# Unread dense 128x128 products between the small tile products of a delta-rule solve

## What is computed

```python
def step(S, inp):
    qt, kt, vt, at, gkt = inp
    Sp = S * jnp.exp(gkt)[..., None]
    u = jnp.einsum('bhk,bhkv->bhv', at, Sp) + vt
    S = Sp + jnp.einsum('bhk,bhv->bhkv', kt, u)
    o = jnp.einsum('bhk,bhkv->bhv', qt, S)
    return (S, o)
```

## Time and profile before

| | us |
|---|---|
| median of 3 runs (lowest 2097.86, highest 2100.38) | 2097.92 |
| the profiled execution's own time | 2104.22 |
| its span, first to last instruction | 2102.4 |
| PE busy in the span | 1794.7 |
| DVE busy | 1135.7 |
| ACT busy | 661.8 |
| POOL busy | 299.7 |
| mean granted clock of PE, as a share of 2.4 GHz | 0.853 |

### The profile page before, as it was taken

The page is one execution under the profiler, slowest core; times in us unless marked ns, Lnnn a source line. Parts: engine busy times, 40 slices in busy tenths (PEclk is TensorE's granted clock), DMA queues, the critical chain, the costliest instruction groups (busy, mean ns, idle before and its releaser), DMA issues. The chain is left out here.

```text
span 2102.4 us, 50203 instructions
## 1 busy us (share of the span) xinstructions
PE 1794.7 (85%) x21793; PEld 1575.6 (75%) x21793; DVE 1135.7 (54%) x2562; ACT 661.8 (31%) x1296; POOL 299.7 (14%) x302
## 2 busy tenths in 40 slices
PE   5677776899999999999999997788777877677589
PEld 4466665689888999999999995577666766666468
DVE  3745554765555455555555565555255246434885
ACT  3344444423223232322223222433223233222232
POOL 0323222700000000000000003312121121110440
PEclk9789887999999999999999997866576577555589
DMA  3100000100000000001010000000000000001001
GB/s 136 48 2 1 0 0 14 70 1 21 21 21 21 21 21 12 30 3 39 1 41 1 1 1 33 1 2 3 3 2 2 3 3 2 3 3 45 1 1 48
DMA packets 9937, 35.91 MB, mean 17 GB/s; under 512 B 3056, under 2 KB 5896, under 8 KB 7176
## 3 DMA queue, kind: packets, MB, share of 16 engines
q1 hardware_dynamic: 9736, 32.96, 4.5%
HBM read 30.47 MB, written 2.49 MB: 16 GB/s over the span
## 5 line engine op out<-in xcount | busy, mean ns | idle before, releaser
L1042 ACT ACTIVATE hidden<-bank,moe_b 128x512 f32<-128x512 f32 (+1 forms) x320 | 213.3, 668 | 537.1 <-PE bank L934 522.7
L951 PE MATMUL bank<-moe_w2h,hidden_hi 128*128 128x256 f32 x1216 | 345.7, 284 | 0.0
L951 PE MATMUL bank<-moe_w2l,hidden_hi 128*128 128x256 f32 x1216 | 344.1, 283 | 0.0
L951 PE MATMUL bank<-moe_w2h,hidden_lo 128*128 128x256 f32 x1216 | 344.0, 283 | 0.0
L934 PE MATMUL bank<-x_hi,moe_w1h 128*128 128x512 f32 (+1 forms) x640 | 243.7, 381 | 2.8 <-ACT hidden L1042 2.7
L934 PE MATMUL bank<-x_lo,moe_w1h 128*128 128x512 f32 (+1 forms) x640 | 242.5, 379 | 0.0
L934 PE MATMUL bank<-x_hi,moe_w1l 128*128 128x512 f32 (+1 forms) x640 | 242.0, 378 | 0.0
L951 PEld LDWEIGHTS bank<-moe_w2h,hidden_hi 128*128 128x128 f32 x1216 | 233.1, 192 | 5.9 <-DVE residual L1076 4.3
L951 PEld LDWEIGHTS bank<-moe_w2l,hidden_hi 128*128 128x128 f32 x1216 | 233.2, 192 | 1.2
L951 PEld LDWEIGHTS bank<-moe_w2h,hidden_lo 128*128 128x128 f32 x1216 | 233.2, 192 | 0.0
L1076 DVE SCALAR_TENSOR_TENSOR residual<-bank,gates,residual 128x256 f32<-128x256 f32 x152 | 73.4, 483 | 290.4 <-PE bank L951 290.4
(11 more groups left out here) (286 smaller groups left out, 3634.3 us busy)
## 6 DMA issues: line engine op xcount, KB each, us to landing
moe_w<-in_moe_w SPq DMA_DIRECT2D x16, 1024.0 KB, 4.8
patches<-in_patches SPq DMA_DIRECT2D x8, 864.0 KB, 4.6
out<-residual SPq DMA_DIRECT2D x19, 128.0 KB, 1.7
ffn_w<-in_ffn_w SPq DMA_DIRECT2D x2, 1024.0 KB, 6.5
att_w<-in_att_w SPq DMA_DIRECT2D x1, 1536.0 KB, 6.1
delta_w<-in_delta_w SPq DMA_DIRECT2D x1, 1280.0 KB
tok_w<-in_tok_w SPq DMA_DIRECT2D x1, 768.0 KB, 4.1
delta_wvf<-in_delta_wvf SPq DMA_DIRECT2D x1, 272.0 KB
```

What stands on the lines that cost most here:

```text
L951: mm = nc.tensor.matmul(bank[4 + n % 3][:, 0:D], left, right, start=(i == 0), stop=(i == len(passes) - 1))
L1042: nc.scalar.activation(H[:, i % 4, 0:n], bank[i % 4][:, 0:n], ACT.Relu, bias=b1[:, x, f:f + 1]).then_inc(acted, 1)
```

## The change

Function `dense(n)` is new. Where the call has a chunk c, and after every fourth lane (n % 4 == 3), it issues one bf16 product of the 128x128 identity against 208 columns (16 columns of the identity, 13 times over), written into columns 304 to 511 of bank 4, which nothing reads. It is called behind each lane of `first_half`, `remainder` and `second_half` but the last of the 32. Two waits on `d_exp` are new, before `first_half` and before `remainder`.

```diff
+            def dense(n):
+                if c is not None and n % 4 == 3:
+                    nc.tensor.matmul(bank[4][:, CT:512], identb[:, :], spread(identb[:, 0:16], 1, 13),
+                                     start=True, stop=True)
+
             def first_half(j):
                 if z is None:
                     return
+                if c is not None:
+                    pe.wait_ge(d_exp, 3)
                 pe.wait_ge(t_back, 3)
                 for lane in lanes(j):
                     for e in range(2):
...
+                    if lane != lanes(j)[-1]:
+                        dense(lane)
                 mm.then_inc(u1_done, 1)
 
             def remainder(j):
                 if z is None:
                     return
                 pe.wait_ge(u1_back, j + 1)
+                if c is not None:
+                    pe.wait_ge(d_exp, 5)
                 for lane in lanes(j):
...
+                    if lane != lanes(j)[-1]:
+                        dense(lane)
                 mm.then_inc(r_done, 1)
 
             def second_half(j):
...
+                    if lane != lanes(j)[-1]:
+                        dense(lane)
                 mm.then_inc(u2_done, 1)
```

## The result

The changed kernel takes **2201.94 us** (median of 4 runs, 2198.26 to 2203.12) against 2098.77 for the kernel before (2097.86 to 2100.38, one run more than in the table above): 1.049 times as long, 95% interval 1.047 to 1.051, or 103 us more. The forecast was 2183, with 2122 to 2214 as its range. The profiled execution took 2203.12 us, 98.9 more than the one of before.

A forecast was written before the change was run, and what follows sets the result against it. PE alone was taken to bound the kernel from first_half to each call's end. Products of 118 us, less 15 of pauses and 18 of clock, gave 85 over 2104.22: 2189, less 6.3 for the median, 2183 us, range 2122 to 2214.

The forecast's parts named there:

- What bounds: From first_half to the call's end (30 us) PE alone is the path; time added there lengthens the kernel.
- The price of a product: Between tiles at 1.2 GHz: entry 0.15, streaming 0.173, exit 0.13, less a pair's 0.054, 0.40 us; at 2.4 GHz 0.30.
- The pauses for instructions: PE's issue pauses in first_half and remainder, about 15 us in seven calls, would vanish and hide that much.
- The clock: Solve mostly stays at 1.2 GHz; stretches at 2.4 GHz, 5 of 48 groups a call, give back 18 us.
- The sum: Seven calls: 118 us of products, less 15 hidden in pauses, less 18 for the clock: 85 over the profiled 2104.22.
- The waits: New waits on d_exp before first_half and remainder cost nothing; the exponentials end 4.6 and 0.8 us earlier.
- A: Changes of form around dense products cost nothing, only streaming does, 0.173 us each: +36, 2134 us; chance 0.14.
- B: Dense products hold 2.4 GHz through the solve but pay for changes of form: +18, 2116 us; chance 0.09.
- C: The high clock is held through the solve and changes of form are free: -14, 2084 us; chance 0.07.

The follow-up runs named there:

- narrow products: Changed kernel with its 294 full-array products streaming 16 columns instead of 208: 2162.43 us, ratio 1.031 to the kernel before.
- heavy kernel: Changed kernel with five dense products back to back in place of each one: 2253.53 us, a single run.

## Why the prediction was right, and where not

- *What bounds.* Right. PE alone carries this stretch; second_half grew by exactly what its dense products take, 5.6 us.
- *The price of a product.* Right: 0.40 us at 1.2 GHz, and 0.29 (0.30 was said) at 2.4. In the remainder, whose pairs take 0.034 us and not the 0.054 of the sum, it is 0.40 as well (0.67 a group). The decomposition stood the test from both sides: with 16 columns 0.24, with two products 0.17 more, in the tiles' own form nothing where no tile shares its place and 0.14 where one does. What the 0.23 us beside the columns consist of, tiles that must first come to their end or a weight load that cannot be made ahead, no run separates. The rule of the Trainium skill, page "TensorEngine Tiling (Array Packing)", section "Key Properties", that a change of tiling mode drains the engine fits these runs: 0.24 us for a way there and back with 16 columns. The gap of N / 1.2 ns of the Trainium skill, page "TensorE: Matmul & The Clock Gate", section "Back-to-back issue gap", is right for the second of two equal products (0.17 us) and misses the first, by 0.23 us.
- *The pauses for instructions.* Right in size: 3.1 us went from first_half and 11.4 from the remainder in the seven calls. Not foreseen: 2.9 us of `output` went too. My reason, that supply catches up, agrees with the products in the tiles' form, which take little time and left most of the pauses, and with those of 16 columns, which take 0.24 us and ended nearly all of them.
- *The clock.* This is the term that was mis-sized: 18 us were given back, and 3.5 us came. The count behind it was nearly right: "If 5 of the 48 groups of a call fall into such stretches" makes 35 in seven calls, and 32 of the 294 products ran at 2.4 GHz. But each saves only 0.40 - 0.29 = 0.11 us. The rest of the 18 us was for tiles and decays that run faster in such stretches, and the kernel before had them as well: its first_half has a mean clock of 0.69 to 0.70 in three of seven calls and its remainder 0.74 and 0.77 in two, the changed kernel 0.61 to 0.62 in four and 0.69 in two. That gain was already in the time before, and the sum counted it again.
- *The sum.* Without that term it is 103 us, and 103 was measured, which is partly luck. Between the two profiled executions, over the seven calls, first_half takes 34.9 us more, the remainder 25.1, second_half 38.1, `output` 3.6 less, and the rest about 4 more, where the sum has nothing: 98.6 in all. The products account for 294 x 0.40 - 3.5 = 114, so nearly 20 us were hidden and not 15; 17.4 of them are the pauses.
- *The waits.* Right, within the 5 us that the kernel with the waits alone leaves open.
- *Rivals.* A falls with the narrow products. B and C need the high clock over the tiles, which one product a group never brought in second_half (0.50 in all seven calls), and two brought only for the start of one in seven. The heavy kernel shows that even then it does not pay: the price of B is real, 0.91 us a group. The Trainium skill, page "TensorE: Matmul & The Clock Gate", section "Why this matters for your kernels", asks for a busy TensorE; the changed kernel's 14.10 us busy at 0.50 speak against taking "busy" as the page of the profile counts it.

## What to carry to other kernels

A product that takes the whole array pays for two changes of form when it stands between small tiles, here 0.23 us besides its columns at 1.2 GHz; in blocks of seven the same 294 products cost 28 us where single ones cost 103, in part because the clock rose. To raise TensorE's clock, put unread work where the engine waits for another one anyway, just ahead of full-array or score work on the path, and not between tiles. The tiles themselves gain little from it: with twenty products the remainder still waits 15.7 us for its instructions, against 14.1 before. Find the price of an inserted instruction at the nearest place of the trace where the same neighbours stand side by side.

## What was not expected of the hardware

A 32x32 product of 208 columns took no time at all between tiles that use another place in the array, even where one of them read the same partitions and wrote others: tiles went on 0.04 us behind its start. The same work does not always get the same clock: with five products a group, three first_halves stayed at 0.50 for 22.32 us and three at 1.00 for 13.46, in one execution, and all seven second_halves at 1.00. Twenty products in a wait gave 0.6%, though PE idles afterwards for up to 2.11 us: in all seven calls the clock was still high when the scores came. With ten it had fallen by then in five of seven.
